# Adjacency build of a graph-network kernel: source split into tile and place, weighting moved to ScalarE, block additions to VectorE

## The reference

```python
edge_index = jnp.stack([src, dst])
xn = _layernorm(x, axis=-1)
x = x + gat(xn, edge_index, ...) + linear_attention(xn, ...)
x = x + mixture_of_experts(_layernorm(x), ...)
xn = _layernorm(x, axis=-1)
x = x + gcn(xn, edge_index, edge_weight, ...) + linear_attention_2(xn, ...)
x = x + spline_layers(x, ...)
```

```python
deg = segment_sum(ew, col, num_segments=n) + 1.0
norm = dinv[row] * ew * dinv[col]
agg = segment_sum(norm[:, None] * x[row], col, num_segments=n)
```

## Time and profile before

| | us |
|---|---|
| median of 3 runs | 3164.07 |
| lowest, highest | 3160.25, 3165.71 |
| profiled execution, its own time | 3162.54 |
| span in its trace | 3160.8 |

### The profile page before, as it was taken

How to read it: one execution, slowest core, us unless ns; L and a number is a source line. 1 busy time by engine, 2 the same in 40 slices (tenths; PEclk the granted TensorE clock), 3 DMA queues, 4 the chain that set the end, 5 groups by cost and what they waited for, 6 DMA issues and landing times.

```text
span 3160.8 us, 33593 instructions
## 1 busy us (share of the span) xinstructions
PE 2801.1 (89%) x13527; PEld 1971.8 (62%) x13527; DVE 1612.7 (51%) x2217; ACT 923.6 (29%) x974; POOL 333.0 (11%) x314
## 2 busy tenths in 40 slices
PE   4777899999989889699956989996879999899999
PEld 4777565688876556477743855553457777555555
DVE  8999679889973444311133230004267777522220
ACT  3666310077751232111110011011054444321110
POOL 5556230000000011100030000000000000000000
PEclk9999999999999899799976999997989999999999
DMA  9700431121030301477755100000020100200000
GB/s 248 265 0 0 110 94 59 42 71 57 34 64 6 84 7 52 140 250 261 259 150 115 33 17 0 30 30 29 0 80 27 40 27 29 105 10 10 10 10 10
DMA packets 123619, 226.60 MB, mean 72 GB/s; under 512 B 18535, under 2 KB 91788, under 8 KB 123006
## 3 DMA queue, kind: packets, MB, share of 16 engines
q1 hardware_dynamic: 107746, 178.79, 19.0%
q0 software_dynamic: 15760, 46.20, 4.6%
HBM read 158.92 MB, written 66.01 MB: 71 GB/s over the span
## 4 chain that ended last, share of the span: by engine, by line
PE 72%; DVE 18%; issue 3%; DMA 3%; ACT 2%; DVEq 1%; POOL 1%; SPq 0%; ACTq 0%; POOLq 0%
PE ps L939 20%; PE ps L1283 13%; PE ps L1267 13%; DVE arena L1660 5%; PE ps L1163 4%; PE ps L1129 4%; PE ps L956 4%; PE ps L1175 4%; DVE arena L1790 2%; DVE arena L1791 2%; PE ps L1216 1%; DVE small L1689 1%; PE ps L1208 1%; PE ps L1039 1%; DMA arena<-in_x_dram 1%
## 5 line engine op out<-in xcount | busy, mean ns | idle before, releaser
L939 PE MATMUL ps<-arena 128*125 128x384 f32 x2160 | 719.8, 496 | 28.3 <-DVE arena L2124 12.8
L939 PEld LDWEIGHTS ps<-arena 128*125 128x125 f32 x2160 | 412.4, 192 | 324.7 <-issue 34.5
L1283 PE MATMUL ps<-arena 128*125 128x384 f32 x1280 | 414.5, 488 | 14.2 <-DVE arena L2164 14.2
L1267 PE MATMUL ps<-arena 128*128 128x312 f32 (+1 forms) x1536 | 407.2, 428 | 15.2 <-DVE arena L2164 15.2
L1267 PEld LDWEIGHTS ps<-arena 128*128 128x128 f32 x1536 | 292.5, 191 | 129.6 <-issue 16.8
L1283 PEld LDWEIGHTS ps<-arena 128*125 128x125 f32 x1280 | 241.0, 188 | 187.6 <-issue 16.1
L1295 ACT ACTIVATE arena<-ps 128x750 f32<-128x750 f32 (+4 forms) x175 | 133.2, 792 | 722.0 <-PE ps L939 206.3
L890 PE MATMUL ps<-arena 128*125 128x152 bf16 x3200 | 244.2, 234 | 67.2 <-DVE arena L1660 65.6
L2164 DVE SCALAR_TENSOR_TENSOR arena<-arena 128x1250 f32<-128x1250 f32 (+1 forms) x170 | 231.4, 1383 | 114.5 <-PE ps L1267 110.9
L890 PEld LDWEIGHTS ps<-arena 128*125 128x125 f16 x3200 | 222.8, 138 | 88.6 <-DVE arena L1660 87.7
L1727 DVE SCALAR_TENSOR_TENSOR arena<-ps,arena 125x768 f32<-125x768 f32 x30 | 28.7, 956 | 379.1 <-PE ps L1283 291.9
(11 more groups left out here) (296 smaller groups left out, 2875.2 us busy)
## 6 DMA issues: line engine op xcount, KB each, us to landing
arena<-in_L_ffn_W_dram SPq DMA_DIRECT2D x34, 1152.0 KB, 7.0
xs_rows<-arena SPq DMA_DIRECT2D x1, 30720.0 KB, 99.5
arena<-xs_rows SPq DMA_DIRECT2D x17, 768.0 KB, 7.9
y_rows<-arena POOLq DMA_DIRECT2D x34, 384.0 KB, 3.3
arena<-in_kw_dram SPq DMA_DIRECT2D x24, 512.0 KB, 5.7
arena<-al_dst POOLq DMA_DIRECT2D x18, 625.0 KB, 4.9
arena<-in_kw_dram SPq DMA_DIRECT2D x6, 1536.0 KB, 9.9
arena<-in_x_dram SPq DMA_DIRECT2D x2, 3600.0 KB
```

Source lines behind the costliest of these rows:

```text
L939: mm = pe.matmul(slot(g)[0:TILE, 512 * half:512 * half + HALF], xt[:, k, i * TILE:i * TILE + TILE], w[:, k, :], start=(k == 0), stop=(k == ...
L1267: mm = pe.matmul(slot(g)[:, 512 * b:512 * b + wd_], w[:, r % 2, ORDER[p], o * P:o * P + P], feat[place(f)][:, lo + b * wd_:lo + b * wd_ + ...
L1283: mm = pe.matmul(slot(g)[0:TILE, 512 * b:512 * b + HALF], fv[:, q, :], w2c[m][q][:, b * HALF:b * HALF + HALF], start=(p == 0 and q == 0), ...
```

## The change

The source number is split into tile (`group`, 0 to 9) and place in the tile (`member`, 0 to 124). The stationary matrix of an edge tile is now the one-hot of the place, 125 columns, in four kinds (plain and weighted by each part). The moving matrix is the one-hot of the spot, 38 x tile + offset in the window, 380 columns, the same for all kinds. TensorE multiplies 4 times per edge tile; the count goes to one PSUM bank and the three weight parts add up in another, four blocks in turn. VectorE makes the plain one-hot of 8 tiles in one instruction, the first weighted copy of the even tiles, and the spots; ScalarE makes the other 20 weighted copies of a block with a per-partition scale; VectorE adds both banks of a finished block into CT and WA, two blocks later. GpSimd's part ends with the clearing.

```diff
-RING = 8
+SPOTS = NT * WIN
...
-        iota_src = ecut(625).bitcast(FP16)
+        spots = ecut(SPOTS // 2).bitcast(FP16)
+        within = ecut(64).bitcast(FP16)[:, 0:TILE]
         src_c = ecut(ECOLS)
         dst_c = ecut(ECOLS)
-        w_c = [ecut(ECOLS // 2).bitcast(BF16) for _ in range(3)]
+        w_p = [ecut(ECOLS) for _ in range(3)]
         w_f = ecut(ECOLS)
-        src_n = ecut(SPREAD * NB)
-        far = ecut(NODES // 2).bitcast(FP16)
+        w_16 = ecut(ECOLS // 2).bitcast(BF16)
+        group = ecut(ECOLS)
+        member = ecut(ECOLS)
+        offset = ecut(ECOLS)
         viol = ecut(ECOLS)
-        iota_0 = ecut(WIN)
-        iota_b = ecut(WIN)
+        spot_of = ecut(ECOLS)
+        spot8 = ecut(2 * SPREAD).rearrange("p (b t) -> p b t", b=2)
...
-        stage = xt_r[0:TILE, stage0:stage0 + 2 * NT * KINDS * WIN].rearrange("p (b j k w) -> p b j k w", b=2, j=NT, k=KINDS)
-        oh_src = h_r[:, 0:RING * 625].bitcast(FP16).rearrange("p (s n) -> p s n", s=RING)
-        oh_dst = h_r[:, 5000:5000 + SPREAD * KINDS * WIN].bitcast(BF16)\
-            .rearrange("p (b t k w) -> p b t k w", b=2, t=SPREAD, k=KINDS)
+        rawf = h_r[:, 7040 - 9 * P:7040].rearrange("p (a r e) -> p a r e", a=3, r=3)
+        oh_src = h_r[:, 0:4000].bitcast(BF16).rearrange("p (b t k n) -> p b t k n", b=2, t=SPREAD, k=KINDS)
+        oh_spot = h_r[:, 4000:7040].bitcast(BF16).rearrange("p (b t n) -> p b t n", b=2, t=SPREAD)
...
+            own.step(pool.iota(spots, [[1, SPOTS]], base=0, channel_multiplier=0,
...
+            own.step(pool.iota(within, [[1, TILE]], base=0, channel_multiplier=0,
...
-            def unstage(b, par, done):
...
+            pool.memset(flagf[0:1, 2:3], 0.0).then_inc(ev("cleared"), 1)
...
-            def bank(par, q):
...
-            def edge_tiles(par, n, fresh):
...
+            def bank(s, q):
+                return ps[0:TILE, s, 512 * q:512 * q + SPOTS]
+            def edge_tiles(s, n, fresh):
+                par = s % 2
                 for u in range(SPREAD):
-                    if u < SPREAD - 1:
-                        pe.wait_ge(ev("src_hot"), n * (SPREAD - 1) + (u + 1))
-                    else:
-                        pe.wait_ge(ev("src_hot_act"), n + 1)
-                    s = u % RING
-                    for j in range(NT):
-                        o = KINDS * WIN * (j % 3)
-                        mm = pe.matmul(bank(par, j // 3)[:, o:o + KINDS * WIN], oh_src[:, s, j * TILE:j * TILE + TILE],
-                                       oh_dst[:, par, u, :, :], start=(fresh and u == 0 and j % 3 == 0), stop=False,
-                                       skip_group_check=True)
+                    pe.wait_ge(ev("hot"), n * SPREAD + (u + 1))
+                    pe.wait_ge(ev("hot_act"), n * SPREAD + (u + 1))
+                    for k in range(KINDS):
+                        mm = pe.matmul(bank(s, min(k, 1)), oh_src[:, par, u, k, :], oh_spot[:, par, u, :],
+                                       start=(fresh and u == 0 and k < 2), stop=False, skip_group_check=True)
                     mm.then_inc(ev("tiles_done"), 1)
-            def open_block(par, b):
...
+            def open_block(b):
+                pe.wait_ge(ev("added"), b + 1)
...
             with pe.If(flag == 0):
-                with pe.Fori(0, NB // 2) as bp:
-                    for par in range(2):
-                        b = bp * 2 + par
-                        open_block(par, b)
-                        pe.wait_ge(ev("dst_hot"), b + 1)
-                        edge_tiles(par, b, True)
+                for b in range(4):
+                    open_block(b)
+                    edge_tiles(b, b, True)
+                with pe.Fori(1, NB // 4) as bp:
+                    for s in range(4):
+                        b = bp * 4 + s
+                        open_block(b)
+                        edge_tiles(s, b, True)
...
+            pe.wait_ge(ev("adj_all"), 1)
...
-            def source(col, n):
...
-            def stage_block(par, b, tiles):
...
+            def weighted(par, col, n):
+                act.wait_ge(ev("plain"), n + 1)
+                for u in range(SPREAD):
+                    for k in range(1 - u % 2, 3):
+                        ins = act.activation(oh_src[:, par, u, 1 + k, :], oh_src[:, par, u, 0, :], ACT.Copy,
+                                             scale=w_p[k][:, bass.ds(col + u, 1)])
+                    ins.then_inc(ev("hot_act"), 1)
             with act.If(flag == 0):
-                with act.Fori(0, NB // 2) as bp:
-                    for par in range(2):
-                        source((bp * 2 + par) * SPREAD + (SPREAD - 1), bp * 2 + par)
-                        stage_block(par, bp * 2 + par, SPREAD)
+                with act.Fori(0, NB // 4) as bp:
+                    for s in range(4):
+                        weighted(s % 2, (bp * 4 + s) * SPREAD, bp * 4 + s)
...
-            own.step(dve.tensor_scalar(src_n, ps[:, 0, 0:NB * SPREAD], -1.0, None, ALU.mult))
+            own.step(dve.memset(group, 0.0))
             own.settle()
-            chain(dve.tensor_copy(w_c[0], w_f))
-            chain(dve.tensor_tensor(w_f, w_f, w_c[0], ALU.subtract))
-            chain(dve.tensor_copy(w_c[1], w_f))
-            chain(dve.tensor_tensor(w_f, w_f, w_c[1], ALU.subtract))
-            chain(dve.tensor_copy(w_c[2], w_f))
+            for k in range(3):
+                chain(dve.tensor_copy(w_16, w_f))
+                chain(dve.tensor_copy(w_p[k], w_16))
+                if k < 2:
+                    chain(dve.tensor_tensor(w_f, w_f, w_p[k], ALU.subtract))
+            for t in range(1, NT):
+                chain(dve.scalar_tensor_tensor(out=group, in0=src_c, scalar=float(t * TILE), in1=group,
+                                               op0=ALU.is_ge, op1=ALU.add))
+            chain(dve.scalar_tensor_tensor(out=member, in0=group, scalar=-float(TILE), in1=src_c,
+                                           op0=ALU.mult, op1=ALU.add))
...
-            dve.tensor_scalar(iota_b, iota_0, base[:, 0:1], None, ALU.add).then_inc(ev("next_block"), 1)
+            chain(dve.scalar_tensor_tensor(out=grouped(spot_of), in0=grouped(group), scalar=float(WIN), in1=grouped(offset),
+                                           op0=ALU.mult, op1=ALU.add))
...
-            def destinations(par, col, count, free, b):
...
-            def sources(col, tile0):
...
-            def next_block(b):
...
+            wide = [P, SPREAD, TILE]
+            def sources(par, col, n, done):
+                dve.wait_ge(ev("tiles_done"), done + CREDIT)
+                dve.tensor_tensor(oh_src[:, par, :, 0, :], within.unsqueeze(1).broadcast_to(wide),
+                                  member[:, bass.ds(col, SPREAD)].unsqueeze(2).broadcast_to(wide), ALU.is_equal)\
+                   .then_inc(ev("plain"), 1)
+                dve.wait_ge(ev("plain"), n + 1)
+                even = oh_src[:, par].rearrange("p (t e) k n -> p t e k n", e=2)[:, :, 0]
+                dve.tensor_tensor(even[:, :, 1, :], even[:, :, 0, :],
+                                  w_p[0][:, bass.ds(col, SPREAD)].rearrange("p (t e) -> p t e", e=2)[:, :, 0]
+                                  .unsqueeze(2).broadcast_to([P, SPREAD // 2, TILE]), ALU.mult)
+            def spotted(par, spot):
+                for u in range(SPREAD):
+                    dve.tensor_scalar(oh_spot[:, par, u, :], spots, spot(u), None, ALU.is_equal).then_inc(ev("hot"), 1)
+            def add_block(s, b):
+                at = dve.value_load(basei[0:1, bass.ds(b, 1)], min_val=0, max_val=LAST)
+                c = bass.ds(at, WIN)
+                v = ps[0:TILE, s, :].rearrange("p (k n) -> p k n", k=2)[:, :, 0:SPOTS].rearrange("p k (j w) -> p k j w", j=NT)
+                dve.wait_ge(ev("counted"), b + 4)
+                dve.tensor_tensor(CT[:, :, c], v[:, 0], CT[:, :, c], ALU.add).then_inc(ev("counted"), 1)
+                dve.wait_ge(ev("added"), b + 4)
+                dve.tensor_tensor(WA[:, :, c], v[:, 1], WA[:, :, c], ALU.add).then_inc(ev("added"), 1)
...
+            dve.wait_ge(ev("cleared"), 1)
             with dve.If(flag == 0):
-                with dve.Fori(0, NB // 2) as bp:
-                    for par in range(2):
-                        b = bp * 2 + par
-                        destinations(par, b * SPREAD, b, b * SPREAD - SPREAD + CREDIT, b)
-                        next_block(b)
-                        sources(b * SPREAD, b * SPREAD)
+                for b in range(4):
+                    sources(b % 2, b * SPREAD, b, (b - 1) * SPREAD)
+                    if b >= 2:
+                        add_block(b - 2, b - 2)
+                    spotted(b % 2, lambda u: spot_of[:, b * SPREAD + u:b * SPREAD + u + 1])
+                with dve.Fori(1, NB // 4) as bp:
+                    for s in range(4):
+                        b = bp * 4 + s
+                        sources(s % 2, b * SPREAD, b, b * SPREAD - SPREAD)
```

(63 more changed lines are left out.)

88 lines of the change are left out of this document (15 added, 73 removed).

## The result

| | before | changed |
|---|---|---|
| median, us | 3162.16 (4 runs) | 3111.63 (4 runs) |
| lowest, highest | 3157.56, 3165.71 | 3106.92, 3113.75 |
| profiled execution, its own time | 3162.54 | 3110.99 |

The ratio is 0.9839, with a 95% interval of 0.9821 to 0.9857: 51 us faster, where 59 were forecast. The median lies inside the forecast's range of 3078 to 3135 us.

The account below looks back on a forecast made before the run. VectorE, held up by GpSimd, was taken to bound the adjacency stage; with ScalarE then pacing 40 blocks at 5.95 us, the first transpose moves from 353.54 to 295.3 us: 3162.5 - 58 = 3104, 3105 on the median, range 3078 to 3135.

Parts of the forecast that it names:

- What bound the kernel before: Adjacency stage: VectorE sets the pace at 7.67 us per block, about 2.5 of it from being held up by GpSimd.
- Setup: VectorE's work ahead of the stage's loop: +6.9 us in sum, first comparison at 42.1 us.
- VectorE per block: VectorE's one-hots, weighted copy, spots and PSUM additions in the stage: together 4.7 us per block of 8 edge tiles.
- bounds of 0 and 0.5 for the load: VectorE's new register load from memory, per block: can lie under the weighted copy, 0 to 0.5 us, taken as 0.
- TensorE per block: The stage's 32 matmuls of 380 columns: 0.161 to 0.168 us each, 5.2 to 5.4 us per block.
- ScalarE's scalings: 20 scalings of 125 columns per block, 0.294 us each, 5.9 us; taken as 5.95, the slowest engine's pace.
- The rival in which small scalings don't overlap: Each ScalarE scaling pays its whole 0.388 us: 7.8 us per block, 73 us more, 3178 us; chance 0.07.
- a table load every other block: Listed among what leaves ScalarE's work per block in the stage; counted as gone.
- the margin for waits in 5.95: ScalarE's block: 5.9 us of scalings taken as 5.95, for a wait per block and the loop's branch every fourth block.
- ScalarE's starts over 0.32 us apart: A sign in the stage that would show the forecast wrong; scalings were expected every 0.29 us.
- 7.1 us for VectorE at one column per cycle: VectorE-bound rival's slow case: spots 0.53 us each, 7.1 us per block, 3151 us; the rival's chance 0.16.
- Slower by TensorE's clock: Rival: TensorE at 1.2 GHz in the stage, 10.3 us per block, kernel over 3270 us; chance 0.01.

Follow-up runs that it names:

- the kernel with eight copies: Changed kernel with ScalarE's loop written out, VectorE making the first weighted copy of all eight tiles, ScalarE 16 scalings instead of 20: 3078.20 us, ratio 0.9738.

## Why the prediction was right, and its step that failed

*What bound the kernel before.* Right, and now shown from both sides: without GpSimd's additions VectorE's one-hots are back to 539 ns, and with them the changed kernel is back at 3161. The forecast called 2.5 us per block VectorE's loss. With the loss gone the kernel before won only 1.9 per block, since TensorE's 5.3 and its wait of 0.5 for ScalarE stood behind it.

*Setup.* First comparison at 41.59 us, forecast 42.1. The nine comparisons took 5.3 us, with 5.4 counted.

*VectorE per block.* 4.7 us forecast. The rows at 204 us give 205.88 - 204.53 = 1.35, then 206.81 - 205.88 = 0.93 for the copy with the register load behind it, 0.93 for both additions, and 1.92 for the spots: 5.1. Where no load stands behind it the copy takes 43.43 - 42.83 = 0.60, as forecast, so the load costs 0.33 us there. But up to 134 us it costs 0.7 more, and VectorE needs 5.7 to 5.8, just under ScalarE's pace. That is outside the forecast's bounds of 0 and 0.5 for the load. They were taken from the median of the earlier trace rows; the maximum in the same row, 1047 ns, is of the loads up to 134 us in the kernel before as well (813 to 1047 ns, and 285 to 298 from 140 us on). No run took the transfer away, so that it is what lengthens the load is inferred from their coming and going together. In the changed kernel this cost nothing, as ScalarE was busy throughout; that is luck, since 0.1 us more per block would have made VectorE the bound there. The spots come every (1.92 - 0.317)/7 = 0.229 us, the number forecast, so an f16 input with a bf16 output keeps the rate of the f16 one-hots before. The rule of the Trainium skill ("VectorE: DVE Perf Modes", What auto-detection actually checks) that the prediction named had said so. It asks for more than the prediction tells, a single source and outermost dimensions that are even or equal, and the spots' one-hot has both. The trace agrees: 0.229 us.

*TensorE per block.* 0.162 us per matmul in the kernel with eight copies, with 0.161 to 0.168 forecast. The lower of the two rests on counting an f32 column of the earlier trace rows as two steps, which no row shows by itself.

*ScalarE's scalings.* Forecast 0.294 us from start to start, measured (19.22 - 0.385)/65 = 0.290. The slope between 250 and 1250 columns held down to 125. The rival in which small scalings don't overlap falls: they last 385 ns and follow every 290. The budget in the Trainium skill ("ScalarE: Activation LUTs", Rules for kernel authors), 0.404 us each as an estimate, is 0.11 us too high here; the same page's section on what the table load costs states an overlap of about 93 ns between neighbours, and with that the trace agrees, 385 - 290 = 95.

*The step that failed* stands in the list of what leaves ScalarE: "and a table load every other block". It was counted as gone. It is one load per pass of the loop in both kernels, and the passes only went from twenty to ten. Each costs 1.4 us bare. Together with the first, which waits behind the first one-hots, 14.2 us of the sum were missing. Against this stood a pace taken too high by 0.16 us per block, 6.4 us: half of it the margin for waits in 5.95, half the 0.294 us that were 0.290. That the two errors have opposite signs is luck; without it the forecast would have been off by 14 us. The stage's end came 2.9 us behind ScalarE's last scaling, with 2.2 forecast. So: 14.2 - 6.4 + 0.7 - 0.5 = 8.0, and the first transpose came 8.1 us after the forecast of 295.3. The observation ahead of the result that "ScalarE's starts over 0.32 us apart" would show it wrong did not catch this, since the loads lie between the starts.

*Two sums.* 3164.07 - (353.54 - 295.3) is 3106, not 3105. And 7.1 us for VectorE at one column per cycle is the block without the load; with it, it is 7.6 and 3171 us. Neither changes the range.

*Slower by TensorE's clock.* The clock was 1.00 over the stage. *Waits.* VectorE waits for TensorE 30.8 us, 0.8 per block, forecast "about 1".

## What to carry to other kernels

A busy share of 98% says which engine sets the pace, not that the work on it takes that long: compare the same line's shortest and mean duration, and look at what the other engines do during the long ones. When work moves to an engine that had slack, everything else on that engine's list (table loads, loop ends, first waits) comes into the path with it and has to be counted again as if new; the same load cost nothing in one kernel and 14 us in the other. A duration that is taken over from another engine needs its minimum, median and maximum looked at by stretch of time, and what the rest of the chip did in each. And ask where the next engine stands before taking the full loss for the gain.

## What was not expected of the hardware

- A loop on ScalarE that holds only copies with a scale has an `ACT_TABLE_LOAD` of 1283 ns in each pass, and one in all when it is written out. Who puts it there, and whether another form of the scaling would be without it, was not tried.
- GpSimd's additions (1170 ns each in the mean) stretch a VectorE instruction of 0.31 us to as much as 1.13 us, and leave one with an input in PSUM alone.
- A register load from memory in an engine's queue takes 0.3 us where the DMA engines are idle and 1.0 us where they are busy 97% of the time, in GpSimd's queue before and in VectorE's after. Behind a copy of 500 columns that cost 0.95 us of VectorE's time instead of 0.25.
- VectorE stands idle for 1.79 us a few instructions behind the end of its conditional branch, when only short work is there; no run was made to find out why.
